# Walsh-Hadamard butterflies of a feed-forward stage issued per finished tile instead of after the loop

## The reference

```python
x = x + _layernorm(_L0_attn_ref(_layernorm(x), ...))
def _L0_ffn_ref(x, W1, W2, W3):        # B,S,D,H = 4,2048,2048,8192
    up_gate = jnp.einsum('bsd,hd->bsh', x, W1)
    up_lin  = jnp.einsum('bsd,hd->bsh', x, W3)
    hidden  = jax.nn.silu(up_gate) * up_lin
    hidden  = fwht(hidden)             # Walsh-Hadamard over 8192, / sqrt(8192)
    return jnp.einsum('bsh,dh->bsd', hidden, W2)
x = x + _layernorm(_L0_ffn_ref(_layernorm(x), ...))
```

## Time and profile before

| what | us |
|---|---|
| three runs, slowest core | 10362.88, 11133.23 (median), 11185.31 |
| the profiled execution, slowest core | 10365.79 |
| its span, first to last instruction (core 2) | 10364.1 |
| spans of the eight cores in it | 10297.0 to 10364.1 |
| PE busy / DVE busy in that span | 6749.0 / 2194.6 |

### The profile page before, as it was taken

How to read it: one execution, slowest core, us unless ns; L and a number is a source line. 1 busy time by engine, 2 the same in 40 slices (tenths; PEclk the granted TensorE clock), 3 DMA queues, 4 the chain that set the end, 5 groups by cost and what they waited for, 6 DMA issues and landing times.

```text
span 10364.1 us, 85183 instructions; the slowest of 8 cores (10297.0 to 10364.1 us)
## 1 busy us (share of the span) xinstructions
PE 6749.0 (65%) x28088; PEld 2828.7 (27%) x28652; DVE 2194.6 (21%) x3147; ACT 1484.4 (14%) x2142; POOL 2309.2 (22%) x2926
## 2 busy tenths in 40 slices
PE   1499655454516765717888880788278888807882
PEld 0144222121202321203334330333034333303331
DVE  3211300103132012131000008322210000083222
ACT  2222212112212112110000000122000000001220
POOL 2355266564614654510000000000100000000001
PEclk9799677776757886759999995899589999958996
DMA  3366477674814653412222220233222222202332
GB/s 106 113 204 203 131 221 228 193 226 138 227 69 138 202 167 122 153 69 84 90 89 86 90 84 1 83 93 93 87 81 90 87 88 90 87 2 77 93 92 77
DMA packets 456845, 1205.35 MB, mean 116 GB/s; under 512 B 65216, under 2 KB 196304, under 8 KB 456416
## 3 DMA queue, kind: packets, MB, share of 16 engines
q0 software_dynamic: 189152, 629.33, 19.5%
q1 hardware_dynamic: 267264, 570.54, 16.8%
HBM read 906.01 MB, written 293.60 MB: 116 GB/s over the span
## 4 chain that ended last, share of the span: by engine, by line
PE 47%; DMA 20%; DVE 14%; issue 7%; POOL 6%; ACT 5%; DVEq 0%; POOLq 0%; ACTq 0%; SPq 0%
DMA cw<-w 12%; PE pB L284 5%; PE pB L282 5%; PE pB L280 5%; PE pA L282 5%; PE pA L280 5%; PE pA L284 5%; POOL cwl L229 4%; DVE zbuf L816 2%; DVE zbuf L818 2%; ACT cwh L226 2%; DMA freg<-fs 2%; POOL w_l L148 1%; PE pA L853 1%; PE pB L857 1%
## 5 line engine op out<-in xcount | busy, mean ns | idle before, releaser
L229 POOL TENSOR_TENSOR cwl<-cw,cwh 128x1024 bf16<-128x1024 f32 (+1 forms) x640 | 1110.2, 1735 | 1590.9 <-ACT cwh L226 1587.1
L148 POOL DMA_DIRECT2D fs<-hidf x32 | 17.5, 545 | 5147.2 <-DVE hidf L865 5138.5
L226 ACT CAST cwh<-cw 128x1024 bf16<-128x1024 f32 (+1 forms) x640 | 556.9, 873 | 2461.7 <-DMA cw<-w 1928.9
L280 PE MATMUL pA<-freg,whi 128*128 128x512 bf16 x2006 | 767.8, 383 | 85.7 <-DVE freg L743 83.5
L282 PE MATMUL pA<-freg,whi 128*128 128x512 bf16 x2008 | 770.4, 384 | 13.4 <-DVE freg L743 11.3
L284 PE MATMUL pA<-freg,wlo 128*128 128x512 bf16 x2006 | 769.2, 383 | 2.1
L280 PE MATMUL pB<-freg,whi 128*128 128x512 bf16 x2008 | 762.0, 379 | 2.5 <-issue 0.4
L282 PE MATMUL pB<-freg,whi 128*128 128x512 bf16 x2006 | 761.0, 379 | 2.1
L284 PE MATMUL pB<-freg,wlo 128*128 128x512 bf16 x2006 | 760.5, 379 | 2.2
L280 PE MATMUL pA<-lnhi,whi 128*128 128x512 bf16 x1003 | 420.5, 419 | 469.9 <-ACT xbuf L581 212.3
L777 DVE SCALAR_TENSOR_TENSOR hidf<-pB,sgs 128x512 f32<-128x512 f32 x128 | 88.6, 692 | 2564.5 <-PE pB L284 2564.5
(11 more groups left out here) (252 smaller groups left out, 10724.1 us busy)
## 6 DMA issues: line engine op xcount, KB each, us to landing
cw<-w POOLq DMA_DIRECT2D x256, 512.0 KB, 6.6
whi<-w_h SPq DMA_DIRECT2D x256, 512.0 KB, 3.6
wlo<-w_l SPq DMA_DIRECT2D x256, 512.0 KB, 4.4
w_h<-cwh POOLq DMA_DIRECT2D x256, 256.0 KB, 4.2
w_l<-cwl POOLq DMA_DIRECT2D x256, 256.0 KB, 4.9
cw<-w POOLq DMA_DIRECT2D x256, 256.0 KB, 3.5
whi<-w_h SPq DMA_DIRECT2D x512, 128.0 KB, 2.0
wlo<-w_l SPq DMA_DIRECT2D x512, 128.0 KB, 2.1
```

What stands on the lines that cost most here:

```text
L148: return em.emit(eng, lambda e, o=out_ap, i=in_ap: e.dma_start(out=o, in_=i), waits=list(waits) + selfw, inc=(sem, 16))
L226: t_hi = aop(lambda e, p=p, c=nc_: e.copy(out=cwh[p][:, 0:c], in_=cw[p][:, 0:c]), waits=[t_in] + bz["cwh"])
L229: t_lo = gop(lambda e, p=p, c=nc_: e.tensor_sub(cwl[p][:, 0:c], cw[p][:, 0:c], cwh[p][:, 0:c]), waits=[t_in, t_hi] + bz["cwl"])
L280: top(lambda e, a=lhsT_hi_f(k), b=rhs_hi_f(k), s=first: e.matmul(bank[:], a, b, start=s, stop=False), waits=w0, inc=False)
```

## The change

The six levels of butterflies are no longer a block of their own after the `dh` loop. After tile `dh` has been copied to `zbuf`, `bf_progress(dh)` emits every butterfly that has just become possible: for h = 1, 2, 4, ... as long as `dh`+1 is a multiple of 2h, the h pairs of the block of 2h tiles that ends at `dh`. The pairs, their number (192 a chunk, 384 VectorE instructions) and their two operations are the same; the order is by block and not by level. The spare tile is now `sqs`, since `freg` is still read by the matmuls of the loop. The first use of it waits for the last two instructions of the prologue that used it.

```diff
@@ in the prologue over NT tiles
                     hid_busy[0] = [t1]
+                    sqs_last = [t1, t2]
                     allpr.append([t3, t4])
@@ ahead of the dh loop
+                phys = list(range(NDH))
+                spare_phys = [NDH]
+                def zap(pi):
+                    return tcol(zbuf, pi) if pi < NDH else sqs[:]
+                bf_tok = {i: [] for i in range(NDH)}
+                bf_tok[NDH] = list(sqs_last)
+
+                def bf_progress(j):
+                    h = 1
+                    while h < NDH and (j + 1) % (2 * h) == 0:
+                        base = j + 1 - 2 * h
+                        for i in range(base, base + h):
+                            a, b = i, i + h
+                            pa, pb_ = phys[a], phys[b]
+                            sp = spare_phys[0]
+                            w = bf_tok[pa] + bf_tok[pb_] + bf_tok[sp]
+                            t_s_ = vop(... e.tensor_add(zap(sp), zap(pa), zap(pb)), waits=w)
+                            t_d_ = vop(... e.tensor_sub(zap(pb), zap(pa), zap(pb)), waits=w)
+                            phys[a], spare_phys[0] = sp, pa
+                            bf_tok[phys[a]] = [t_s_]
+                            bf_tok[pb_] = [t_d_]
+                            bf_tok[spare_phys[0]] = [t_s_, t_d_]
+                        h *= 2
@@ in the dh loop, behind the copy of pC to zbuf (t_ze)
                     z_toks[dh] = t_ze
+                    bf_tok[dh] = [t_ze]
+                    bf_progress(dh)
@@ behind the dh loop
-                (zap with zspare, and the same pairs level by level:
-                 while h < NDH: for base in range(0, NDH, 2 * h): for i in ...)
```

More of the change, by code:

```diff
@@ L752, in build_nc @@
                 last_w13 = []
+                phys = list(range(NDH))
[13 more added lines that the diff above has]
+                            w = bf_tok[pa] + bf_tok[pb_] + bf_tok[sp]
+                            t_s_ = vop(lambda e, sp=sp, pa=pa, pb=pb_: e.tensor_add(
+                                zap(sp), zap(pa), zap(pb)), waits=w)
+                            t_d_ = vop(lambda e, pa=pa, pb=pb_: e.tensor_sub(
+                                zap(pb), zap(pa), zap(pb)), waits=w)
+                            phys[a], spare_phys[0] = sp, pa
[3 more added lines that the diff above has]
+                        h *= 2
                 for dh in range(NDH):
@@ L798, in build_nc @@
                 lnpair_done = last_w13
[L800 to L824, removed]
                 out_banks = [pA, pB, pC, pD]
```

## The result

| | kernel before | changed kernel |
|---|---|---|
| runs, slowest core: lowest | 10362.88 | 10053.22 |
| median | 11159.27 (10 runs) | 10703.85 (8 runs) |
| highest | 11355.92 | 10926.84 |
| ratio of the runs at full clock | | 0.9701 (95% interval 0.9673 to 0.9729) |

The change makes the kernel 3.0% faster. The measured median, 10,704 us, lies outside the forecast's 10,025 to 10,155. Nine further runs of the changed kernel are on record, from 10146.25 to 11067.21 us with a median of 10870.49. In most executions of either kernel some cores get a lower TensorE clock in the feed-forward block, and the median is one of those; the ratio compares only the runs in which no core does.

A forecast was written before the change was run, and what follows sets the result against it. TensorE bounds the dh loop, VectorE's butterflies the 270 us behind it. Per chunk 180.7 - 1.6 - 23.2 - 2.3 - 1.4 = 152.2 us, two chunks 304 us off 10365.79: 10,061 us, range 10,025 to 10,155.

The forecast's parts named there:

- rival D: Dense loop: VectorE's work beside TensorE on all cores lowers the granted clock; 10,709 us, 3.3% slower; chance 3%.
- its own signs: In the dh loop: granted clock below 0.98 means Rival B or rival D; growth over 40 us means prediction wrong.
- (a): In the dh loop, 1, 3 and 7 pairs take at most 10.4 us of 20.79 and cost nothing.
- Rival A: VectorE is slower beside TensorE, a pair taking 2.1 us: 10,153 us, still 2.1% faster; chance 6%.
- (b): Behind tiles 15 and 47, 15 pairs need 21.6 us: L777 0.8 us late, twice, 1.6 us a chunk.
- (c): Behind tile 31, 31 pairs need 44.0 us: L777 of tile 32 is 23.2 us late and TensorE stands.
- (d): Behind the last copy, 63 pairs need 88.8 us before L842; TensorE's wait falls 180.7 us, to about 90.
- (e): In the dh loop, TensorE's climb to full clock behind stall (c): 11 matmuls at 0.21 us extra, 2.3 us.
- (f): In the dh loop, TensorE's two gaps of 3.3 us in (b) may lose the clock: 0.7 us each, 1.4 in sum.
- Rival B: The clock falls in every gap of the loop, costing 179 us: 10,240 us, 1.2% faster; chance 4%.
- Rival C: The change doesn't do what it says; butterflies all queue behind the loop: 10,366 us; chance 2%.

The follow-up runs named there:

- e_zero2: Changed kernel with feed-forward activations and the bf16 copies of W1, W3 and W2 set to zero: 10,003 to 10,283 us, median 10,206 (4 runs).
- e_end: Changed kernel with new pair order and spare tile kept, but all 192 pairs emitted after the dh loop: ratio to before 1.004.
- e_none: Changed kernel with all butterflies left out, so its output is another one: lowest run 9826.29 us, ratio to before 0.947.
- e_load: Changed kernel plus ten VectorE adds behind each tile except every 16th: block 5338 to 5344 us, lowest run 10102.64 us.
- run 310: Not a run's label: 310 is the us that the lowest run lost, 10053.22 us for the changed kernel against 10362.88 before.
- e_spread: Changed kernel with butterflies queued, at most 14 pairs behind a tile, queue emptied behind tile 63: lowest run 10029.49 us, block 53 us less.

## Why the prediction was right or wrong

**The time: wrong, by the level it was made for.** The step that failed is the sentence "no row covers those longer ones, and I forecast for an execution like the profiled one". Two of three runs of before had shown that such an execution was the rarer case. The range should have covered the other, or the central value should have been put there. The trace of the changed kernel shows what it is. Matmuls of core 5 in the `dh` loop, timeline, and the table of the stretch they lie in, with a PEclk of 0.81:

```profile
5500.01 0.43 PE L280 MATMUL pB<-freg,whi 128*128 128x512 bf16 x1
5500.27 0.44 PE L282 MATMUL pB<-freg,whi 128*128 128x512 bf16 x1
...
5500.00:5502.00 2.00, 2.00 (x9) 0.87 (x8) 0.00 (x0) 0.00 (x0) 0.00 (x0) 0.81 0.00 0
```

They start 0.262 us apart in the mean instead of 0.2155, which is 0.82 of the speed. Turns of the loop on core 5, VectorE:

```profile
5129.41 0.69 DVE L806 SCALAR_TENSOR_TENSOR hidf<-pB,sgs 128x512 f32<-128x512 f32 x1 [23.19 <-PE pB L284]
...
5159.12 0.69 DVE L806 SCALAR_TENSOR_TENSOR hidf<-pB,sgs 128x512 f32<-128x512 f32 x1 [25.90 <-PE pB L284]
...
5187.53 0.69 DVE L806 SCALAR_TENSOR_TENSOR hidf<-pB,sgs 128x512 f32<-128x512 f32 x1 [20.38 <-PE pB L284]
```

They last 29.71 and 28.41 us in turn, 29.06 in the mean, against 23.83 on core 1: in two loops of 63 turns up to 126 x 5.23 = 659 us, and stage 4 adds 6,144 x 0.047 = 289 us, when it lasts all through. On core 5 it set in at 5006 us, and its block took 6106 us, 765 more than the 5341. The 1.3 us more in every other turn are a fall of the clock in the gap. Core 6 had it in the attention block, from 308 us on, and in the loop of chunk 0 until 6028 us, and ended at 10,351 us.

The trace of before held the level too, outside of the rows that the prediction used. Core 2 in the attention block, table by stretch:

```profile
4366.00:4377.00 11.00, 8.50 (x32) 3.16 (x30) 1.99 (x3) 1.31 (x3) 3.55 (x6) 0.81 0.30 95
```

On cores 0 to 3 such stretches add up to 195 to 257 us, all ahead of the feed-forward block. So it could have been seen before the change was run that this level exists on these cores.

The Trainium skill, page "TensorE: Matmul & The Clock Gate", Part 1, tells of a peak-current limiter that takes a die with three or more cores in dense matmuls to 13/16 of the clock, and says that zero operands do not trip it. The granted clock of 0.81 and the spacing on core 5 agree with 13/16 (0.265 us is my estimate from the page's figure); that it grips whenever all cores are dense does not (in the profiled execution of before all eight ran both loops without it, and in this one cores 6 and 7 left it at 6028 us while 4 and 5 kept it); nor do zero operands keep it away: e_zero2, zeros on both sides, has the stretch at 0.81 shown above. I had cited this rule and dismissed it, by the one execution that I had a trace of, and had made it rival D, a thing that VectorE's work might cause.

**Is it rival D after all?** The low level is there without the change, so VectorE's work in the loop is not what brings it about. Whether that work makes it more frequent stays open. Runs with all cores near full clock (within 80 us of the kernel's full-clock time) were 9 of 47 of before (3 of 10, 2 of 15, 4 of 11 and 0 of 11 in the four sets), 3 of 10 of e_end and 3 of 8 of e_none; of the kernels with butterflies inside the loop, 2 of 17 and 0 of 8 (changed), 1 of 7 (e_load), 1 of 6, 0 of 8, 1 of 7 and 1 of 6 (the others). That is 15 of 65 without them and 6 of 59 with them; chance alone gives a difference as large in about one case of eleven, by my estimate. The medians point neither way: that of before lies 796, 846, 723 and 858 us over 10,363 in the four sets, that of the changed kernel 647 (729 over all 17) and 890 over 10,057. So D in this weaker form is neither supported nor excluded. What decides in which execution, on which cores and for how long the level comes was not found.

By its own signs the prediction failed on cores 4 to 7 too: there the clock in the loop of chunk 0 fell below 0.98, and the loop took 242 to 280 us more than 63 turns of 23.83 us, over the 40 allowed. On cores 0 to 3 that was 32 to 35 us, against 3 to 7 before.

**The change: right, and to a few us.** The forecast was 304 us; on cores at full clock the block lost 305, and the lowest run 310. The two waits gave back 361 us, as forecast, and the two loops took 55 us of that back (mean of cores 0 to 3 against the eight of before), where 57 were forecast.

- *Rhythm of a pair, (a)*: 1.40 us beside matmuls, turns with 1, 3 or 7 pairs at 23.83 us, but for a few falls of the clock. Rival A does not hold; e_load excludes it for 470 us more of work a chunk.
- *(b)*, 15 pairs: the turns behind tiles 15 and 47 lasted 24.98 and 24.64 us (core 1), 1.15 and 0.82 us more; 0.8 was forecast. (0.35 of the 1.15 are one longer pause between two pairs.)
- *(c)*, 31 pairs: forecast 44.0 us from copy to L777, measured 43.99; turn 47.03 - 23.83 = 23.2 us more, as forecast. e_spread took it away: 53 us, where 54 were expected of (b), (c) and the climbs. On a core at the low level (c) is smaller, since the cover is longer: 47.07 - 29.06 = 18 us on core 5.
- *(d)*, 63 pairs: wait 90.1 us, forecast 90.
- *(e)* mis-sized: the climb behind (c) took 7 slow matmuls (core 1, chunk 0), not 11, and cost 1.3 us in the next turn (25.15 us), not 2.3; on cores 0 to 3 it cost 1.3 to 1.6 us.
- *(f)*: the gap behind tile 15 of chunk 0 was 3.66 or 3.67 us on cores 0 to 3, for that pause, and lost the clock on all four. Of the other gaps behind 15 pairs, recorded at 3.30 to 3.33 us, one did (core 3, chunk 1). Each fall cost 1.7 us in the turn behind (25.51). Over all 16 gaps that is 0.5 us in the mean, where 0.7 was taken.
- *(e) and (f) together*: on cores 0 to 3 the turns of chunk 0 exceeded 23.83 us by 32.1 to 35.3 us in sum, of which (b) and (c) are 25.2, and those of chunk 1 by 27.0 to 31.4 us, of which they are 24.8. That leaves 7 to 10 and 2 to 7 us for climbs and small losses; before it was 3 to 7 in either loop. Forecast was 3.7 us a chunk on top of before; the mean is 2.4.
- *Rival B*, a fall in every gap, did not come: at full clock cores 0 to 3 had 4 to 6 falls in the loop of chunk 0 and 1 to 4 in that of chunk 1, the one behind (c) among them; before there were one to three a loop. (Its 179 us are 1.4 us for 128 gaps, not for 126. And the 1493 us in the last paragraph of the prediction are the length of a window; 63 turns of 23.83 us take 1501.)
- *Rival C* is excluded by the timeline, and e_end shows what it would have looked like.

## What to carry to other kernels

Work that an idle engine does behind a dense loop can be emitted inside it, at the earliest point where its inputs are ready; count it against the cover of one turn, since only the surplus shows: here 7 pairs of 1.40 us were free, and 14 in e_spread, while 31 cost 23 us. Cap what is emitted per turn, and let the next stage ask for the results in the order in which they come ready: the two together brought another 212 us, and nearly all that leaving the work out would bring. And if the runs of the kernel before lie at two levels, say for which of them the forecast is, and give the range for what will be measured.

## What the runs showed of the hardware

- VectorE adds of 128x512 float32 beside back-to-back matmuls of TensorE slow neither: 692 ns each, and turns of 23.83 us with 570 more of them.
- There is a level of the matmuls between the two of the clock: a granted clock of 0.81 and 0.262 us from start to start for 512 columns, against 0.2155 and some 0.42. Cores of one die can differ in it (4 and 5 against 6 and 7), it may begin or end in the middle of a loop (5006 us on core 5, 6028 us on core 6), and it depends on the values: the median run lies 647 us over the full-clock time with data, 149 with zeros on both sides in the feed-forward block, on another chip.
- At that level the short gaps of 2.5 us lose the clock in about every other turn (29.71 and 28.41 us); at full level 1 to 6 falls were counted in 63 turns.
